# Reordering TensorE's work in two loops of a graph network kernel, and unpacking window words at once

## The reference, cut to what matters

```python
# L0: attention over the edges, summed at the source node (4 heads)
e = leaky_relu(a_src[:, src] + a_dst[:, dst] + fc_b[0], 0.2)
e = exp(e - seg_max.T[:, src])
msg = e / seg_sum ... * hp[:, dst, :]
out = segment_sum(msg, src).mean(axis=0) + bias

# L2: a radial network gives every edge its own small matrices
R = relu(abs_distances[:, None] @ w1 + b1) @ w2 + b2       # 64 hidden, 384 outputs
Y = spherical_harmonics(rel_vec)
acc = acc + NORM[i] * einsum('euv,ef,evi,ofi->euo', R[..., k], Y[f], Fj, C)
out = zeros.at[dst].add(msg)
```

## Time and profile before

| | |
|---|---|
| median of 3 runs | 23471.85 us (23463.01 to 23507.63) |
| profiled execution, its own time | 23492.08 us |
| span in the profile | 23490.1 us |
| mean granted TensorE clock | 0.619 |
| busy share of the span | PE 45%, DVE 74%, ACT 21%, POOL 63% |

### The profile page before, as it was taken

How to read it: one execution, slowest core, us unless ns; L and a number is a source line. 1 busy time by engine, 2 the same in 40 slices (tenths; PEclk the granted TensorE clock), 3 DMA queues, 4 the chain that set the end, 5 groups by cost and what they waited for, 6 DMA issues and landing times.

```text
span 23490.1 us, 291216 instructions
## 1 busy us (share of the span) xinstructions
PE 10598.4 (45%) x63545; PEld 8169.3 (35%) x63546; DVE 17306.3 (74%) x23890; ACT 4973.9 (21%) x12809; POOL 14896.0 (63%) x14067
## 2 busy tenths in 40 slices
PE   0132101000017777733235777777777764225422
PEld 0122101000016666632224555555555543224321
DVE  8999999999346666643666888888888875654565
ACT  0000000000002222233002444444444444003300
POOL 0058888788747777774775777777655521770376
PEclk6555555555557777755556777777777765555555
DMA  2011111211211111167332000001100046235524
GB/s 46 0 18 24 23 26 24 30 23 27 32 40 29 29 29 29 27 131 151 75 75 25 11 11 11 11 11 11 11 10 10 10 93 186 69 68 144 153 69 63
DMA packets 1837588, 1095.95 MB, mean 47 GB/s; under 512 B 988876, under 2 KB 1789101, under 8 KB 1836077
## 3 DMA queue, kind: packets, MB, share of 16 engines
q0 software_dynamic: 454272, 412.11, 11.9%
q1 hardware_dynamic: 886268, 362.30, 6.4%
q10 hardware_dynamic: 496944, 320.42, 5.7%
HBM read 700.94 MB, written 391.12 MB: 46 GB/s over the span
## 4 chain that ended last, share of the span: by engine, by line
POOL 22%; PE 21%; DVE 20%; issue 16%; DVEq 10%; DMA 6%; ACT 3%; ACTq 1%; SPq 1%; POOLq 0%
POOL gat L738 18%; PE banks L1322 7%; DVEq L2292 5%; PE banks L1184 5%; POOL srcs L758 5%; DMA dsts<-key_rows 4%; DVE hot L2010 3%; DVE srcs L2287 3%; DVE red L2293 3%; PE banks L1309 2%; ACT srcs L929 2%; DVE arena L1640 2%; PE banks L1190 2%; DVE arena L2021 1%; DVEq L484 1%
## 5 line engine op out<-in xcount | busy, mean ns | idle before, releaser
L738 POOL DMA_INDIRECT gat<-tab,nbr x3328 | 4276.3, 1285 | 2337.0 <-DMA nbr<-nbr_src 1323.2
L758 POOL DMA_INDIRECT srcs<-spread,nbx x2808 | 3118.3, 1110 | 2836.2 <-DMA nbx<-from_src 1717.9
L738 POOL DMA_INDIRECT gat<-tab,pay x3328 | 3169.5, 952 | 1072.4 <-issue 891.8
L704 POOL DMA_INDIRECT pay<-records,nbr x2784 | 3125.9, 1123 | 1090.7 <-issue 847.7
L1322 PE MATMUL banks<-w2rows,dsts 128*128 128x384 f32 x6656 | 3447.0, 654 | 129.6 <-DVE srcs L2287 115.8
L2293 DVE TENSOR_REDUCE red<-srcs 128x80 f32<-128x1280 f32 x1664 | 2473.7, 1487 | 151.4
L1184 PE MATMUL banks<-srcs,hot 128*128 128x96 bf16 (+1 forms) x11232 | 1150.0, 279 | 2939.2 <-DMA srcs<-spread,nbx 2630.8
L1113 PE MATMUL banks<-ident,arena 128*128 128x128 f32 x2240 | 430.3, 379 | 4531.8 <-DVE arena L1641 4505.2
L2021 DVE TENSOR_TENSOR arena<-arena,banks 128x96 f32 (+2 forms) x4472 | 1208.5, 270 | 1519.3 <-issue 1025.9
L1640 DVE TENSOR_TENSOR arena<-arena 128x1024 f32<-128x1024 f32 (+3 forms) x1548 | 2086.3, 1348 | 80.5 <-issue 5.6
L1641 DVE TENSOR_TENSOR arena<-arena 128x1024 f32<-128x1024 f32 (+3 forms) x1548 | 2099.4, 1356 | 0.0
(11 more groups left out here) (377 smaller groups left out, 19941.6 us busy)
## 6 DMA issues: line engine op xcount, KB each, us to landing
spread<-srcs SPq DMA_DIRECT2D x936, 192.0 KB
dsts<-key_rows SPq DMA_DIRECT2D x936, 128.0 KB
spread<-srcs ACTq DMA_DIRECT2D x468, 204.0 KB
staged<-gat ACTq DMA_DIRECT2D x416, 148.0 KB, 1.8
gat<-staged ACTq DMA_DIRECT2D x416, 148.0 KB
dsts<-key_rows ACTq DMA_DIRECT2D x468, 128.0 KB
gat<-tab,nbr POOLq DMA_INDIRECT x3328, 2.6
gat<-tab,pay POOLq DMA_INDIRECT x3328, 2.4
```

Source lines behind the costliest of these rows:

```text
L704: pool.indirect_dma_start(out=pay[:, s, t, :], out_offset=None, in_=records, in_offset=bass.IndirectOffsetOnAxis(ap=nbr[:, s, t:t + 1], ax ...
L738: pool.indirect_dma_start(out=gatv(s, GC[pas])[:, t, :], out_offset=None, in_=TAB[pas], in_offset=bass.IndirectOffsetOnAxis(ap=row, axis=0 ...
L758: pool.indirect_dma_start(out=chunk_rows(s, c)[:, q, :], out_offset=None, in_=rows, in_offset=bass.IndirectOffsetOnAxis(ap=nbx[:, s, q:q + ...
```

## The change

- PE, radial: the order of a step was part 0, `weight_rows`, sum 0, part 1, sum 1, hidden 0, part 2, sum 2, hidden 1, part 3, sum 3. It becomes part 0, `weight_rows`, part 1, sum 0, part 2, hidden 0, sum 1, part 3, sum 2, hidden 1, sum 3.
- ACT, radial: the copy of sum 0 moves from ahead of the geometry copies to behind them.
- PE, attention: the transposes of step n + 1 come ahead of the sums of step n - 1; the sums take banks 0 and 1 or 2 and 3 in turn.
- DVE, attention: the sums are added two steps behind and not one; the one-hots are made two steps ahead; ahead of the messages there is a wait until the sums of the step before are made.
- ACT, attention: the loads for the step after next are issued at the end of a step.
- `group_windows`: all four fields are put into registers right behind the load.

```diff
-            word = eng.snap(word)
-            return [((word >> (WIN_BITS * q)) & ((1 << WIN_BITS) - 1)).with_bounds(min_val=0, max_val=W - 1) for q in range(groups)]
+            fields = [((word >> (WIN_BITS * q)) & ((1 << WIN_BITS) - 1)).with_bounds(min_val=0, max_val=W - 1) for q in range(groups)]
+            for field in fields:
+                eng.to_reg(field)
+            return fields
...
             def attention_step(i, s, final):
                 n = i * SLOTS + s
-                if not (final and s >= 2):
-                    attention_loads(i + (s + 2) // SLOTS, (s + 2) % SLOTS)
                 act.wait_ge(logit_ready, n + 1)
                 s_.activation(prob[:, :, :], logit[:, :, :], ACT.Exp).then_inc(prob_ready, 1)
                 if not (final and s == SLOTS - 1):
 
                     act.wait_ge(am_ready, n + 1)
                     attention_transposes(n + 1, s + 1)
+                if not (final and s >= 2):
+                    attention_loads(i + (s + 2) // SLOTS, (s + 2) % SLOTS)
...
                 if not first:
-                    keep_sums(n - 2, 0, wins[0])
                     act.wait_ge(msg_ready, n + (STEPS - 1))
...
                 if not first:
-                    keep_sums(n - 2, 1, wins[1])
-                    keep_sums(n - 2, 2, wins[2])
+                    for q in range(GPS - 1):
+                        keep_sums(n - 2, q, wins[q])
...
-                           lambda q: bank[q // 2][:, (q % 2) * CM:(q % 2 + 1) * CM], GPS)
+                           lambda q: bank[2 * (s % 2) + q // 2][:, (q % 2) * CM:(q % 2 + 1) * CM], GPS)
 
             def att_step(i, s, first, more):
                 n = i * SLOTS + s
+                if more:
+                    att_transposes(n + 1, (s + 1) % SLOTS)
                 if not first:
                     att_sums(n - 1, (s - 1) % SLOTS)
                 if more:
-                    att_transposes(n + 1, (s + 1) % SLOTS)
                     att_nodes(n + 1, (s + 1) % SLOTS)
...
                     if more and p == 0:
                         weight_rows(n + 1, (s + 1) % SLOTS)
-                    if not first:
-                        radial_sums(n - 1, (s - 1) % SLOTS, p, wins[p])
-                    if more and p in (1, 2):
-                        hidden(n + 1, p - 1)
+                    if more and p == 2:
+                        hidden(n + 1, 0)
+                    if not first and p > 0:
+                        radial_sums(n - 1, (s - 1) % SLOTS, p - 1, wins[p - 1])
+                    if more and p == 3:
+                        hidden(n + 1, 1)
+                    if not first and p == 3:
+                        radial_sums(n - 1, (s - 1) % SLOTS, 3, wins[3])
...
                 if more:
-                    i1, s1 = after(i, s)
-                    one_hot(key_att, i1, s1, hot4[s1]).then_inc(hot_ready, 1)
-                if not first:
-                    att_sums(n - 1, wins)
+                    s2 = (s + 2) % SLOTS
+                    one_hot(key_att, i + (s + 2) // SLOTS, s2, hot4[s2]).then_inc(hot_ready, 1)
+                if behind == 2:
+                    att_sums(n - 2, s - 2, wins)
+                if behind:
+                    dve.wait_ge(sums_ready, n)
                 dve.wait_ge(prob_ready, n + 1)
```

More of the change, by code:

```diff
@@ L2036, in _, with att_sums, att_step @@
             dve.drain()
-            def att_sums(n, wins):
-                add_sums(wins, CM, lambda q: bank[q // 2][:, (q % 2) * CM:(q % 2 + 1) * CM], 0, n)
-            def att_step(i, s, first, more):
+            def att_sums(n, s, wins):
+                add_sums(wins, CM, lambda q: bank[2 * (s % 2) + q // 2][:, (q % 2) * CM:(q % 2 + 1) * CM], 0, n)
+            def att_step(i, s, behind, more):
                 n = i * SLOTS + s
-                if not first:
-                    wins = windows(win_att, n - 1, GPS)
+                if behind == 2:
+                    wins = windows(win_att, n - 2, GPS)
                 dve.wait_ge(am_ready, n + 1)
@@ L2069, in att_step @@
                                 ALU.mult).then_inc(msg_ready, 1)
-            one_hot(key_att, 0, 0, hot4[0]).then_inc(hot_ready, 1)
+            for s in range(2):
+                one_hot(key_att, 0, s, hot4[s]).then_inc(hot_ready, 1)
             for s in range(SLOTS):
-                att_step(0, s, s == 0, True)
+                att_step(0, s, min(s, 2), True)
             with dve.Fori(1, ITERS - 1) as i:
                 for s in range(SLOTS):
-                    att_step(i, s, False, True)
+                    att_step(i, s, 2, True)
             for s in range(SLOTS):
-                att_step(ITERS - 1, s, False, s < SLOTS - 1)
-            att_sums(STEPS - 1, windows(win_att, STEPS - 1, GPS))
+                att_step(ITERS - 1, s, 2, s < SLOTS - 2)
+            for s in range(SLOTS - 2, SLOTS):
+                att_sums(STEPS - SLOTS + s, s, windows(win_att, STEPS - SLOTS + s, GPS))
             dve.drain()
```

## The result

The changed kernel takes 22692.49 us (median of 4 runs, 22690.34 to 22700.49) against 23477.22 for the kernel before in the same comparison: 785 us less, ratio 0.9665, 95% interval 0.9648 to 0.9681.

A forecast was written before the change was run, and what follows sets the result against it. DVE, busiest beside POOL but not full, was taken to wait for PE's products and sums, with POOL's `collect` capping attention's gain. Radial -390 and attention -200 made -590 us: 22,880 us, range 22,740 to 23,150.

The forecast's parts named there:

- the slack of 250 us ahead of `chunk_gather(0)`: Between attention's `collect` and the next layer: POOL stood still 250.21 us, all a shorter attention stage could give.
- rival 1: Attention: POOL doesn't hold the gain back, all 455 us arrive; -845 us in all, 22,627 us; chance 0.05.
- POOL's hold: Behind attention: `collect` ends at 10936 us and sets the next layer's start, so 198 us arrive, not 455.
- That loss goes with the number of DVE instructions, not with time.: Attention: gathers of `collect` beside DVE lose a fixed 0.96 us a step, 399 us in all.
- 1.385 us: Stage behind attention: time for each of the 366 gathers displaced there, 507 us together.
- the prediction's own 0.11: Attention: beyond a gain of 226 us, each further microsecond gained takes back 0.11.
- 0.07 us a step for long low spells: Radial: 30 us put back against the 418.1 us of waits removed, giving -390 us.
- The bound of 474 from whole steps: Radial: most that could be gained, if every step took 14.44 us and not 15.58.
- Rival 2: Radial: clock still falls in PE's two short idles, half of 390 us lost; -395 us, 23,077 us; chance 0.18.
- Rival 4: Radial: TensorE's clock stays low throughout, 16.5 us a step; 183 us slower in all, 23,655 us; chance 0.04.
- rival 3: Attention: PE at low clock sets the step; -60 us in place of -200, -450 in all, 23,022 us; chance 0.07.
- The moves priced at nothing: ACT's later copy of sum 0, POOL's radial work of 14.13 us, ACT's attention loads: each expected to cost nothing.

The follow-up runs named there:

- e3: The kernel before with only `group_windows` changed, fields put into registers right behind the load: 23168.93 us, ratio 0.9868.
- e1: The kernel before with only the radial reordering on PE and ACT: 23068.79 us, ratio 0.9827.
- e2: The kernel before with only the attention part (PE, DVE and ACT order, banks), fields worked out where used: 23198.71 us, ratio 0.9882.
- e4: The kernel before, old radial order, with four extra matmuls a step in PE's idle time ahead of the wait for the messages: 22984.42 us, ratio 0.9788.
- e8: The changed kernel with LATE_ITERS 20 instead of 17, the radial order of before and four extra matmuls a step: 22537.76 us, ratio 0.959.
- e7: The changed kernel with LATE_ITERS 20 instead of 17, moving 96 gathers of `collect` to the radial stage: 22575.66 us, ratio 0.9608.

## Why the prediction was off

**The reading of the bound was right.** The radial stage was short of the second product at a low clock, and the slack of 250 us ahead of `chunk_gather(0)` was what the attention stage could give before POOL held it back. Both show in the trace after, and rival 1 (all of it arrives) is out: of 628 us, 354 arrived, and POOL was idle ahead of the first L760 for only the 5 us of a load. Of the 209 us between the forecast of 590 and the 799 between the spans, 156 come from how POOL's hold was sized and 54 from the radial stage.

**The step that failed: "That loss goes with the number of DVE instructions, not with time."** It was fixed at 0.96 us a step, worked out from one step length. It is the rest of the step behind whole gathers, and at 5.67 us it is 0.67: 416 x 0.29 = 121 us less, in which 97 gathers were made that would have taken 1.385 us each behind the stage: 134 us. A second piece is the tail: I priced all displaced gathers at 1.385 us, as beside the spread stage, but that stage was over 279 us before `collect`, and 223 of them took 1.25: some 30 us. `collect` also began 10 us earlier (6669.0 against 6678.6). Against that, attention gained 173 us more than forecast, which by the prediction's own 0.11 takes back 19 us, and POOL waited 5 us for a load. That is about 150 us, for the 156 between 198 expected and 354 measured.

**Attention itself: 628 us, not 455.** The step is 5.67, not 6.13. I priced the unpacking on DVE alone (131 us) and PE's part at nothing, though L1199 carries as many ALU_OPs; e3 gives 0.61 us a step for both. This error cost little, since by the prediction's own sum a gain in the stage above some 226 us is held back anyway.

**Radial: 444 us, not 390; mechanism right, size off.** I put back 0.07 us a step for long low spells; measured are 61.8 us of wait, so the waits gave 356 us. But the sum took only that row. Ahead of the same line, idle time put down to "issue" fell by 42 us (113.8 to 72.1). And over 415 steps DVE's busy time fell from 5670 to 5616 us, with the means of the large groups within 6 ns of before: where DVE doesn't wait, an instruction starts 0.08 to 0.09 us before the one ahead of it ends (L2287 at 16008.63, L2282 until 16008.71), and a stand loses that overlap. The stands went from 559 to 121, by which I estimate some 39 of the 54 us. The bound of 474 from whole steps held it; the row of waits understated it. And 59 us of the 444 appear only together with the unpacking (e1; e2 leaves the stage unchanged), which I had at nothing here. Beside the old order the unpacking gives 25 us (e3), and beside the fill nothing (14.42 us a step in e4, 14.43 in e8).

**The clock.** I named the fallen clock and the place of part 1 as one cause; e4 parts them. At full clock the order costs nothing. The new order does not keep the clock up throughout (0.84 to 0.85 in the radial stretch, from 0.76): it makes low spells nearly harmless. Rival 2 assumed that the short idles would let the clock fall again. The clock does fall behind them, as the 2.76 us part shows, but with parts 3 to 5 us early this costs 62 us and not 195. The Trainium skill ("TensorE: Matmul & The Clock Gate", section "A second HAM failure mode: psum-queue depth-cycling") says that short idles between groups of matmuls let the clock swing; this trace agrees. Rival 4 (clock low throughout) and rival 3 (PE sets the attention step) did not come about; L2075 waited 2.5 us for PE.

**The moves priced at nothing** held: no wait on loads is seen in attention, the copy of a sum (L979) holds TensorE's next sum up by 0.6 us at most (0.34 at 15013.64 us; 121 us in 351 times), where TensorE is early, and POOL's round with late gathers stays under the step, even with 12 more of them (e7).

The range was too narrow on its lower side because POOL's hold was taken as a cap with no spread. Its own uncertainty, a loss a step between 0 and 1.25 us over 416 steps, was some 500 us wide.

## What to carry to other kernels

When a stage gets shorter, look for the engine that works beside it and is not due until the stage behind: its slack, read as idle time ahead of its next work, is what can be gained. If one engine blocks another once a loop, the loss depends on how the loop's length divides by the other's beat, so don't carry it over as a constant; try a longer step too. And before moving work to hide a slow spell of TensorE, fill its idle time with matmuls into a bank about to be overwritten: it says in one run whether the clock is the cause, and may be the better kernel (here by 84 us).

## What the runs showed of the hardware

- An indirect gather on GpSimd that begins inside a DVE instruction with two inputs from SBUF ends 0.82 us behind the end of that instruction, if that is later than its own 0.94 us. So for L2075 above and the one-hots (L2016): from 7500 to 9200 us of the changed kernel, 600 gathers began inside one of them with more than some 0.1 us left, and ended 0.80 to 0.84 us behind it. The long updates between the stages do the same, with the longest gathers of the region. A gather that begins first isn't held: in the kernel before, from 7500 to 9800 us, 480 gathers began up to 0.94 us ahead of L2066 or L2010 and took 0.94 to 0.96 us.
- The `tensor_scalar` of the spread stage (L2113, 0.75 us) holds a gather in the same way that begins more than some 0.1 us inside it (110 gathers, 0.80 to 0.83 us behind). But it also holds one that began 0.1 to 0.45 us ahead of it, until 0.12 us behind its own end (63 gathers, 0.11 to 0.13); the cast L2104 lets a gather go in the same way. DVE and POOL in the changed kernel, in four places:

```profile
8410.29 1.23 DVE L2016 TENSOR_TENSOR srcs<-iota,key_att 128x1024 f32<-128x1024 f32 x1
...
8411.07 1.26 POOL L706 DMA_INDIRECT pay<-records,nbr  x1 [0.30 <-issue]
...
9441.01 1.90 DVE L2104 CAST arena<-arena 128x3332 bf16<-128x3332 f32 x1
9442.98 3.63 DVE L2106 TENSOR_TENSOR arena<-arena 128x3332 bf16<-128x3332 f32 x1
...
9437.66 5.37 POOL L706 DMA_INDIRECT pay<-records,nbr  x1 [0.30 <-issue]
9443.33 4.09 POOL L706 DMA_INDIRECT pay<-records,nbr  x1 [0.30 <-issue]
...
9459.57 0.75 DVE L2113 TENSOR_SCALAR hotT<-dsts,lanes 128x1024 bf16<-128x1024 uint8 x1 [2.66 <-DMA dsts<-key_rows]
...
9459.28 1.16 POOL L706 DMA_INDIRECT pay<-records,nbr  x1 [0.30 <-issue]
...
9465.96 0.75 DVE L2113 TENSOR_SCALAR hotT<-dsts,lanes 128x1024 bf16<-128x1024 uint8 x1 [2.12 <-DMA dsts<-key_rows]
...
9466.21 1.32 POOL L706 DMA_INDIRECT pay<-records,nbr  x1 [0.30 <-issue]
```

  Ends, POOL against DVE: 8412.33 and 8411.52 (one-hot), 9447.42 and 9446.61 (L2106), 9443.03 and 9442.91 (cast), 9460.44 and 9460.32 (L2113 begun behind the gather), 9467.53 and 9466.71 (L2113 begun ahead of it). The Trainium skill ("SBUF — State Buffer", section "Who interferes with whom") has a DVE instruction with two SBUF inputs contend with GpSimd instructions that read SBUF, and casts and `tensor_scalar` block GpSimd fully when they run in a two-port mode, the one that issues first going first. The traces agree for gathers that begin inside the instruction; that L2113 also holds a gather begun ahead of it differs from that order, and here the measurement decides.
- Adds with one input from PSUM (L2027) and memsets cost a gather nothing: beside the memset of 10.92 us (L2041) nine gathers took 0.94 to 0.95 us each.
- Four extra matmuls a step raised the granted clock of a 6 ms stretch from 0.76 to 1.00 and made the kernel 493 us faster (e4).
- Moving seven register instructions a step on each of DVE and PE out from between dependent work shortened the attention stage by 252 us (e3, whose edit reaches all users of `group_windows` and gave 309 in all).
